# Pairs 0 and 1 share one seven-product T in the opening of an attention kernel on TensorE

## The chip, the cores and the metric

The kernel runs on one core of a Trainium2 chip. The metric is the device time of one execution in microseconds (us). TensorE multiplies, VectorE, ScalarE and GpSimd do the elementwise work, and SyncE issues the transfers.

## What is computed

```python
output = einsum('bni,io->bno', x, weight)              # x: (32, 256, 512) float32
q, k   = einsum('bni,io->bno', x, wq), einsum('bni,io->bno', x, wk)
alpha  = einsum('bno,bmo->bnm', q, k)
alpha  = softmax(maximum(alpha, 0) * (adj != 0), axis=1)
x      = layernorm(x + einsum('bnm,bmo->bno', alpha, output))
```

The kernel never forms q and k. It makes G = Wq Wk^T once, T = G x for each pair of batch elements, the scores x T, and V = x W.

## The kernel before

**Pairs, halves, splits.** The 32 batch elements are worked on as 16 pairs (a tile holds 2 x 256 rows). Each float32 operand is split into a rounded part `hi` and a rest `lo`, and a product is three matmuls: hi hi, hi lo, lo hi. The `hi` is a copy by ScalarE; the `lo` is a subtraction by VectorE (`rest`, line 1026) or GpSimd.

**Seven products.** A T or a V of 512 x 512 is made of 2 x 2 blocks by a seven-product scheme (`P1` to `P7`, each in two halves of six matmuls). It needs sums of x blocks (`xs`, S1 to S4, summed by GpSimd), their splits (`s_hi`, `s_lo`), sums of blocks of G (`T1` to `T3`, `D4`) or W, and sums over PSUM banks (`copy_t` on ScalarE, `sum_t` on VectorE).

**The loop.** From pair 2 on, a group works on two pairs. `fill_t` makes T for both at once: the x operand has 512 columns, 256 of each pair. Then come the output of the pair before, the scores of the first, its V, the scores of the second, the output of the first, and the second's V.

**The opening, which the change rewrites.** TensorE's list is: seven warm-up matmuls; `fill_first_v` (three of four rows of pair 0's V); `fill_g` (48 matmuls of 512 columns); `fill_first_t` (pair 0's T without the seven products: 48 matmuls of 512 columns); the fourth row of V; the scores of pair 0 (48 of 256 columns); `fill_second_t` (pair 1's T by seven products: 84 matmuls of 256 columns); the output of pair 0; the scores of pair 1; `fill_v(1)`; then the loop.

**The order on the other engines** is a list written out by hand for each engine. An engine runs its list strictly in order, and a semaphore wait at one operation holds back all behind it. The lists that matter here:
- ScalarE: splits of Wq and Wk, of V, of G, of x1 (pair 1's x) and its sums, of G's sums, of T; exponents of pair 0; copies of the second T among the roundings of p; T's splits; splits of pair 2's x and sums; exponents of pair 1; copies of V.
- VectorE: the rests of Wq and Wk, of V, of G, G's sums (`sum_gt`), their rests, T's, then masks and maxima, p's rests, the residuals of pair 0.
- GpSimd: waits for the last rest of Wk, then four x sums of pair 1, four rests of its x, four rests of its sums, four sums of W and their rests; four x sums of pair 2, its eight rests.
- SyncE: x0, W, Wq, Wk, the four blocks of x1 once x0 is split, adj; later x for the residual and pair 2.

Of the kernel before, what the change touches and what calls it, by code (L numbers as in the profile page):

```python
# [5 lines left out]
ALU = mybir.AluOpType  # L6
# [21 lines left out]
          (P5, 0): 9, (P5, 1): 10, (P3, 0): 11, (P3, 1): 12, (P4, 0): 13, (P4, 1): 14}  # L28
V_DONE = {(P1, 0): 1, (P1, 1): 2, (P7, 0): 3, (P6, 0): 4, (P6, 1): 5, (P7, 1): 6, (P5, 0): 7, (P5, 1): 8,
# [17 lines left out]
FIRST_A, FIRST_S = (A11, A21, A12, A22), (S3, S2, S1, S4)  # L47
# [6 lines left out]

B11, B12, B21, B22, T1, T2, T3, D4 = range(8)
W_ORDER = (T1, T3, T2, D4)
G_PLACE = {B11: 0, B21: 1, B22: 2, T1: 3, T2: 4, T3: 5, D4: 6}
# [3 lines left out]
def gnn_resnorm(nc: bass.Bass, x, x0_t, x_t, adj_t, w, wq_t, wk_t, out):  # L61
# [14 lines left out]
    with ExitStack() as ctx:  # L76
# [65 lines left out]
        wk_hi, wk_lo = a_hi[:, 1], a_lo[:, 1]  # L142
# [6 lines left out]
        b12 = parts[:, 0, 0]  # L149
# [16 lines left out]
        ring = [chain[:, 0], chain[:, 1], bank_y[:, 0], bank_y[:, 1]]  # L166
# [3 lines left out]
        g_bank = [o_bank[0], o_bank[1], o_bank[2], bank_z]  # L170
# [4 lines left out]
        xt_loaded, zeros_ready = sems("xt_loaded", 4), sem("zeros_ready")  # L175
# [13 lines left out]

        t_filled, t_copied, t_summed, c12_copied = sem("t_filled"), sem("t_copied"), sem("t_summed"), sem("c12_copied")  # L190
        v_filled, v_copied, v_summed = sem("v_filled"), sem("v_copied"), sem("v_summed")
        t0_filled, t_hi_ready, t_lo_ready = sem("t0_filled"), sem("t_hi_ready"), sem("t_lo_ready")
# [28 lines left out]
        def _(sp):  # L221
# [7 lines left out]
            def load_a(i, u):  # L229

                sp.wait_ge(x_summed[1], 4 * i - 4 + READ_BY[u])
                if u in B_LO_FIRST:
                    sp.wait_ge(b_lo_ready, 2 * i - 4 + B_LO_FIRST[u])
                else:
                    sp.wait_ge(a_lo_ready[1], 2 * i + A_LO[1][u])
                load_block(2 * i, u)

            def load_b(i, u):
                sp.wait_ge(x_summed[0], 4 * i - 4 + READ_BY[u])
                sp.wait_ge(a_lo_ready[0], 4 * i + A_LO[0][u])  # L240
                load_block(2 * i + 1, u)
# [76 lines left out]
        def _(pe):  # L318
# [16 lines left out]
            def t_half(i, c, pairs):  # L335
                to = {P2: bank_z[:, pairs], P7: bank_y[:, c, pairs], P4: bank_y[:, c, pairs]}.get(i, chain[:, c, pairs])
# [18 lines left out]
            def fill_t(i):  # L355
# [6 lines left out]
                def x_split(u):  # L362
                    pe.wait_ge(a_lo_ready[0], 4 * i + A_LO[0][u])
                    if u in B_LO_FIRST:
                        pe.wait_ge(b_lo_ready, 2 * i - 2 + B_LO_FIRST[u])
                    else:
                        pe.wait_ge(a_lo_ready[1], 2 * i + 2 + A_LO[1][u])

                def xs_split(s):
                    pe.wait_ge(s_lo_ready[0], 4 * i - 4 + S_LO[0][s])  # L370
                    pe.wait_ge(s_lo_ready[1], 4 * i + S_LO[1][s])
# [38 lines left out]
            def fill_second_t():  # L410

                def x_split(u):
                    pe.wait_ge(a_lo_ready[1], FIRST_A.index(u) + 1)

                def xs_split(s):
                    pe.wait_ge(s_lo_ready[1], FIRST_S.index(s) + 1)

                one = slice(1, 2)
                pe.wait_ge(gt_lo_ready, 4)
                xs_split(S3)  # L420
                t_half(P7, 0, one)
                x_split(A11)
                t_half(P1, 0, one)
                t_half(P1, 1, one)
                x_split(A12)
                t_half(P2, 0, one)
                t_half(P7, 1, one)
                pe.wait_ge(t_summed, 1)
                t_half(P2, 1, one)
                pe.wait_ge(t_copied, 1)  # L430
                xs_split(S2)
                t_half(P6, 0, one)
                pe.wait_ge(t_copied, 2)
# [12 lines left out]
                x_split(A22)
                t_half(P4, 0, one)
                pe.wait_ge(t_summed, 4)
                t_half(P4, 1, one)
# [57 lines left out]
            def fill_last_of_first_v():  # L507

                pe.wait_ge(gt_summed, 8)
# [5 lines left out]
            def g_chunk(j, k):  # L515
                half, cols = j // 2, slice(j % 2 * P, (j % 2 + 1) * P)
                return add_chunk(g_bank[j][:], (wq_hi[:, k, half, cols], wq_lo[:, k, half, cols]),
# [13 lines left out]

            def g_parts(k, j):
                kk, cols = k % 2, slice(j % 2 * P, (j % 2 + 1) * P)
                if k < 2 and j >= 2:
                    return p_hi[:, kk, cols], p_lo[:, kk, cols]
                b = G_PLACE[k // 2 * 2 + j // 2]
                return g_hi[:, b, kk, cols], g_lo[:, b, kk, cols]

            def fill_first_t():

                for k in range(K):
                    pe.wait_ge(g_lo_ready, (2, 4, 5, 6)[k])
                    h, kk = k // 2, k % 2
                    for j in range(K):
                        if k == 0 and j < R - 1:
                            pe.wait_ge(v_lo_ready, j + 1)
                        last = add_chunk(ring[j], g_parts(k, j), (a_hi[:, 0, h::2, kk], a_lo[:, 0, h::2, kk]),
                                         k == 0, k == K - 1)
                        if k == K - 1:
                            last.then_inc(t0_filled, 1)  # L550
# [20 lines left out]

            def fill_s_b(i):
# [4 lines left out]
                pe.wait_ge(a_lo_ready[1], 2 * i + 2 + A_LO[1][A21])  # L577
# [13 lines left out]
            def fill_o_b(i, first=False):  # L591

                p = 0 if first else 2 * i - 1
                for g in range(2):
                    pe.wait_ge(p_lo_ready, R * p + M * g + M)
                    if first:
                        pe.wait_ge(v_lo_ready, 4)
                    else:
                        pe.wait_ge(v_lo_ready, R * p + (V_AT[1][A11], 4)[g])
                        if g == 0:  # L600

                            pe.wait_ge(added, R * p)
                    for n in range(M):
                        if M * g + n == 3:
                            pe.wait_ge(added, R * p + 1)
                        fill_row(M * g + n, o_bank[(M * g + n) % 3][:])

# [65 lines left out]
        def _(act):  # L673
            def split_a(i, slot, u, first=False):

                act.wait_ge(xt_loaded[u], 32 * i + 16 * slot)
                if first:
                    act.wait_ge(s_filled, 2)
# [7 lines left out]
            def split_s(i, slot, s, first=False):  # L686
                act.wait_ge(x_summed[slot], 4 * i - 4 + 4 * slot + S_SUMMED[s])
# [15 lines left out]
            def copy_second_t(product):  # L703
                for c in range(2):
                    act.wait_ge(t_filled, T_DONE[product, c])
                    nc.scalar.copy(parts[:, PART[product], c, 1], chain[:, c, 1]).then_inc(t_copied, 1)
# [6 lines left out]
            def split_t_a(i, u):  # L713
                if u == A11:

                    act.wait_ge(s_filled, 4 * i)
# [8 lines left out]
            def copy_c12(i):  # L725

                act.wait_ge(squared, R * (2 * i - 1))
                nc.scalar.copy(c12_b[:], chain[:, :, 1]).then_inc(c12_copied, 1)

            def split_t_b(i, u):  # L730

                act.wait_ge(s_filled, 4 * i + 1 + u // 2)
                if u == A12:
                    act.wait_ge(c12_copied, i)
                whole = c12_b[:] if u == A12 else parts[:, BLOCK_AT[u], :, 1]
                nc.scalar.copy(t_hi[:, u], whole).then_inc(t_hi_ready, 1)

            def split_second_t(u):
                if u == A12:
                    act.wait_ge(t_filled, T_DONE[P3, 1])  # L740
                    whole = chain[:, :, 1]
                else:
                    act.wait_ge(t_summed, {A11: 2, A22: 4, A21: 6}[u])
                    whole = parts[:, BLOCK_AT[u], :, 1]
# [180 lines left out]
            def split_g(j):  # L925

                act.wait_ge(g_filled, j + 1)
                if j < 2:
                    nc.scalar.mul(g_hi[:, G_PLACE[B11], j], g_bank[j][:, 0], -1.0).then_inc(g_hi_ready, 1)
                    nc.scalar.mul(p_hi[:, j], g_bank[j][:, 1], -1.0).then_inc(g_hi_ready, 1)  # L930
                    if j == 0:
                        act.wait_ge(qk_lo_ready, 2 * K)
                    nc.scalar.mul(b12[:, j], g_bank[j][:, 1], -1.0).then_inc(b12_copied, 1)
                else:
                    b = G_PLACE[B21]
                    nc.scalar.mul(g_hi[:, b:b + 2, j - 2], g_bank[j][:], -1.0).then_inc(g_hi_ready, 1)
# [616 lines left out]
```

## Time and profile before

| | |
|---|---|
| time, median of 3 runs | 523.15 us (523.07 to 523.55) |
| the profiled execution's own time | 522.93 us |
| its span, first to last instruction | 521.1 us |
| TensorE busy | 511.5 us (98%), 3259 matmuls |
| VectorE, ScalarE, GpSimd busy | 370.8, 325.7, 257.4 us |
| mean granted TensorE clock | 0.996 of full |

The span is the time in which the profiler saw instructions; 1.8 us of the execution's time lie around it. Matmuls overlap, so the distance of their starts, not their duration, is what one costs.

### The profile page before, as it was taken

To read this page: it belongs to the slowest core of one execution; us is meant where nothing else is said; L and a number is where in the kernel's file an instruction comes from. 1 tells how busy PE (TensorE), PEld (TensorE's weight loads), DVE (VectorE), ACT (ScalarE), POOL (GpSimd) and SP (SyncE) were. 2 spreads that over 40 slices of the span, in tenths; PEclk is the share of its full clock that TensorE was granted. 3 is DMA by queue.
4 is the path that set the end of the run, shared out by engine and by line. 5 is a ranking of instruction groups with operands and counts; after the bars stand their busy time and mean duration, and the time that the engine had idled before them with its cause. 6 is when DMAs were issued, how large, how long until landed. Compare 5 with 4: busy or idle time off the path is not lost.

```text
span 521.1 us, 9934 instructions
## 1 busy us (share of the span) xinstructions
PE 511.5 (98%) x3259; PEld 466.4 (90%) x3259; DVE 370.8 (71%) x746; ACT 325.7 (62%) x747; POOL 257.4 (49%) x196
## 2 busy tenths in 40 slices
PE   8999999999999999999999999999999999999994
PEld 6889998899989998899988999889998999889994
DVE  5667845776948677586866778577684867757686
ACT  6566556386763857649474677638686385764583
POOL 0396974339535377145661486333952537810011
PEclk9999999999999999999999999999999999999998
DMA  8305231034330616024350343405251061502334
GB/s 304 140 1 192 79 136 61 21 141 143 129 134 20 221 61 241 20 65 177 122 199 20 121 141 128 154 20 182 100 200 61 20 221 60 201 1 67 135 135 187
DMA packets 30735, 62.05 MB, mean 119 GB/s; under 512 B 2048, under 2 KB 3072, under 8 KB 30720
## 3 DMA queue, kind: packets, MB, share of 16 engines
q1 hardware_dynamic: 30576, 61.61, 33.0%
q10 hardware_dynamic: 144, 0.26, 0.2%
q8 instruction: 7, 0.11, 0.1%
q14 instruction: 8, 0.07, 0.0%
HBM read 45.09 MB, written 16.78 MB: 119 GB/s over the span
## 4 chain that ended last, share of the span: by engine, by line
PE 95%; DVE 2%; ACT 1%; DMA 1%; issue 0%; POOLq 0%; POOL 0%; DVEq 0%; ACTq 0%
PE o_bank L320 12%; PE o_bank L321 12%; PE o_bank L322 12%; PE chain L320 11%; PE chain L322 11%; PE chain L321 11%; PE bank_y L320 6%; PE bank_y L321 6%; PE bank_y L322 6%; PE bank_z L320 3%; PE bank_z L322 3%; PE bank_z L321 3%; DMA xt<-in_x_t 1%; PE chain L502 0%; PE chain L503 0%; ACT v_hi L755 0%
## 5 line engine op out<-in xcount | busy, mean ns | idle before, releaser
L1442 POOL TENSOR_TENSOR s_lo<-xs,s_hi 128x512 fp32r<-128x512 f32 x60 | 82.0, 1384 | 35.4 <-ACT s_hi L692 35.4
L1437 POOL TENSOR_TENSOR a_lo<-xt,a_hi 128x512 fp32r<-128x512 f32 x42 | 58.3, 1396 | 61.5 <-ACT a_hi L684 61.5
L322 PE MATMUL o_bank<-t_hi,a_lo 128*128 128x256 f32 x256 | 72.4, 283 | 0.0
L321 PE MATMUL o_bank<-t_lo,a_hi 128*128 128x256 f32 x256 | 72.4, 283 | 0.0
L320 PE MATMUL o_bank<-t_hi,a_hi 128*128 128x256 f32 x256 | 72.4, 283 | 0.0
L1433 POOL TENSOR_TENSOR xs<-xt 128x512 f32<-128x512 f32 x30 | 39.1, 1318 | 45.6 <-DMA xt<-in_x_t 29.3
L1447 POOL TENSOR_TENSOR rstd<-var_eps,minus_half 128x4 f32<-128x4 f32 x14 | 14.2, 1015 | 92.6 <-DVE var_eps L1123 92.6
L711 ACT COPY parts<-chain 128x256 f32<-128x256 f32 x90 | 33.1, 369 | 39.6 <-PE chain L322 38.4
L320 PE MATMUL chain<-w_hi,s_hi 128*128 128x256 f32 x180 | 51.0, 284 | 0.5 <-ACT parts L711 0.5
L321 PE MATMUL chain<-w_lo,s_hi 128*128 128x256 f32 x180 | 50.9, 283 | 0.0
L322 PE MATMUL chain<-w_hi,s_lo 128*128 128x256 f32 x180 | 50.9, 283 | 0.0
L1026 DVE TENSOR_TENSOR v_lo<-parts,v_hi 128x512 fp32r<-128x512 f32 x45 | 48.8, 1097 | 0.9 <-ACT v_hi L755 0.9
L321 PEld LDWEIGHTS o_bank<-t_lo,a_hi 128*128 128x128 f32 x256 | 49.1, 192 | 0.3
L320 PEld LDWEIGHTS o_bank<-t_hi,a_hi 128*128 128x128 f32 x256 | 49.1, 192 | 0.3
L322 PEld LDWEIGHTS o_bank<-t_hi,a_lo 128*128 128x128 f32 x256 | 49.1, 192 | 0.0
L1038 DVE TENSOR_TENSOR parts<-parts,bank_y 128x512 f32<-128x512 f32 (+1 forms) x32 | 20.7, 653 | 39.2 <-ACT parts L701 26.1
L320 PE MATMUL o_bank<-v_hi,p_hi 128*128 128x512 f32 (+1 forms) x126 | 48.5, 385 | 0.0
L321 PE MATMUL o_bank<-v_lo,p_hi 128*128 128x512 f32 (+1 forms) x126 | 48.5, 385 | 0.0
L322 PE MATMUL o_bank<-v_hi,p_lo 128*128 128x512 f32 (+1 forms) x126 | 48.4, 384 | 0.0
L1109 DVE SCALAR_TENSOR_TENSOR xn<-o_bank,xn 128x512 f32<-128x512 f32 x60 | 41.0, 685 | 8.0 <-PE o_bank L322 8.0
L1129 DVE TENSOR_SCALAR xn<-xn,neg_mean,rstd 128x512 f32<-128x512 f32 x56 | 39.4, 725 | 10.1 <-POOL rstd L1447 10.1
L701 ACT COPY parts<-chain 128x512 f32<-128x512 f32 x42 | 24.6, 587 | 35.0 <-PE chain L322 34.4
(222 smaller groups left out, 1633.7 us busy)
## 6 DMA issues: line engine op xcount, KB each, us to landing
xt<-in_x_t SPq DMA_DIRECT2D x64, 256.0 KB, 3.1
xn<-in_x SPq DMA_DIRECT2D x16, 1024.0 KB, 5.2
out<-xn SPq DMA_DIRECT2D x14, 1024.0 KB, 6.0
adj<-in_adj_t SPq DMA_DIRECT2D x16, 512.0 KB, 5.5
xn<-in_wq_t SPq DMA_DIRECT2D x4, 256.0 KB, 5.2
parts<-in_wk_t SPq DMA_DIRECT2D x4, 256.0 KB, 5.2
out<-xn SPq DMA_DIRECT2D x2, 512.0 KB, 2.8
out<-xn SPq DMA_DIRECT2D x4, 256.0 KB, 2.3
```

What stands on the lines that cost most here:

```text
L320: nc.tensor.matmul(dst, a[0], b[0], start=first, stop=False, skip_group_check=shared)
L321: nc.tensor.matmul(dst, a[0], b[1], start=False, stop=False, skip_group_check=shared)
L322: return nc.tensor.matmul(dst, a[1], b[0], start=False, stop=last, skip_group_check=shared)
L701: nc.scalar.copy(parts[:, PART[product], c], chain[:, c]).then_inc(t_copied, 1)
L711: nc.scalar.copy(parts[:, PART[product], c, 0], chain_v[:, c]).then_inc(v_copied, 1)
L1026: return nc.vector.tensor_tensor(dst, whole, hi.bitcast(F32), ALU.subtract)
L1038: nc.vector.tensor_tensor(part, part, bank, ALU.add).then_inc(t_summed, 1)
L1109: nc.vector.scalar_tensor_tensor(out=xn[:, slot, r], in0=row.rearrange("q j n -> q (j n)"), scalar=1.0, in1=xn[:, slot, r], op0=ALU.mult, ...
L1129: nc.vector.tensor_scalar(xn[:, slot, r], xn[:, slot, r], neg_mean[:, r:r + 1], rstd[:, r:r + 1], ALU.add, ALU.mult).then_inc(normed, 1)
L1433: nc.gpsimd.tensor_tensor(xs[:, s], a, b, op).then_inc(x_summed[slot], 1)
L1437: nc.gpsimd.tensor_tensor(a_lo[:, slot, u], xt[:, u], a_hi[:, slot, u].bitcast(F32), ALU.subtract).then_inc(a_lo_ready[slot], 1)
L1442: nc.gpsimd.tensor_tensor(s_lo[:, slot, s], xs[:, s], s_hi[:, slot, s].bitcast(F32), ALU.subtract).then_inc(s_lo_ready[slot], 1)
```

## The change

Pair 0's dense T and pair 1's separate T go. Pairs 0 and 1 become the first group: one seven-product T of 84 matmuls of 512 columns, as in the loop. The rest of the opening follows the loop's order: scores of pair 0, the fourth row of V, scores of pair 1, output of pair 0, `fill_v(1)`. To feed it:
- pair 1's x lands in `soft` and a part of `parts`, behind Wk and with no wait; Wk's split is kept in pair 1's `s_hi`, `s_lo`; G's fourth row is in a half of `bank_y`, which leaves `bank_z` free;
- GpSimd makes x sums of both pairs from the sixth of the eight rests of Wq and Wk on; VectorE takes six of the rests that were GpSimd's (`split_first_b`, `split_first_s`);
- P2's second half goes to `o_bank0` in place of waiting for `bank_z`;
- the extra rounding of G's B12 (`p_hi`, `p_lo`) goes; G's last row is split as soon as it is filled, and G's sums and their splits are in the order T3, T2, T1, D4;
- pair 2's x is loaded, summed and its sums are rounded sooner: on ScalarE the four `split_s(1, 0, ...)` stand ahead of pair 1's `split_t_b`, and the roundings of its blocks stand between those of p.

```diff
+T_FIRST = {**T_DONE, (P1, 0): 1, (P1, 1): 2, (P2, 0): 3, (P2, 1): 4, (P7, 0): 5, (P7, 1): 6}
-FIRST_A, FIRST_S = (A11, A21, A12, A22), (S3, S2, S1, S4)
+FIRST_A, FIRST_S = (A11, A12, A22, A21), (S3, S1, S2, S4)
+FIRST_LO = {S3: 1, S2: 2}, {S1: 1, S4: 2}
+G_ORDER = (T3, T2, T1, D4)
...
+            def fill_first_t():
...
+                both = slice(0, 2)
+                pe.wait_ge(g_lo_ready, 2)
+                pe.wait_ge(b_lo_ready, B_LO_FIRST[A11])
+                pe.wait_ge(v_lo_ready, 2)
+                t_half(P1, 0, both)
+                t_half(P1, 1, both)
+                pe.wait_ge(g_lo_ready, 4)
+                pe.wait_ge(gt_summed, 1)
+                pe.wait_ge(b_lo_ready, B_LO_FIRST[A12])
+                t_half(P2, 0, both)
+                t_half(P2, 1, both, o_bank[0][:])
+                pe.wait_ge(gt_lo_ready, G_ORDER.index(T3) + 1)
+                xs_split(S3)
+                pe.wait_ge(v_lo_ready, 3)
+                t_half(P7, 0, both)
+                pe.wait_ge(gt_summed, 8)
+                t_half(P7, 1, both)
+                pe.wait_ge(t_copied, 1)
+                pe.wait_ge(gt_lo_ready, G_ORDER.index(T2) + 1)
+                xs_split(S2)
+                t_half(P6, 0, both)
...
+                pe.wait_ge(t_copied, 3)
+                pe.wait_ge(gt_lo_ready, G_ORDER.index(T1) + 1)
+                xs_split(S1)
+                t_half(P5, 0, both)
...
+                pe.wait_ge(t_copied, 5)
+                xs_split(S4)
+                t_half(P3, 0, both)
...
@@ TensorE's list @@
             fill_g()
             fill_first_t()
+            fill_first_s()
             fill_last_of_first_v()
-            pe.wait_ge(t_lo_ready, 4)
-            fill_scores(0, 0)
-            fill_scores(0, 1)
-            fill_second_t()
-            fill_o_b(0, first=True)
...
+            fill_s_b(0)
+            fill_first_o()
             fill_v(1, 1, first=True)
@@ ScalarE's list, the new one @@
+            split_first_a(A11)
+            split_first_s(0, S3)
+            split_first_a(A12)
+            split_g(0)
+            split_g(1)
+            split_first_s(0, S1)
+            split_first_s(0, S2)
+            split_first_a(A22)
+            split_first_a(A21)
+            split_g(2)
+            split_first_s(1, S3)
+            split_g(3)
+            split_gt(T3)
+            split_gt(T2)
+            split_first_s(1, S1)
+            copy_first_t(P1, 0)
+            copy_first_t(P1, 1)
+            split_first_s(0, S4)
+            split_first_s(1, S2)
+            split_gt(T1)
+            split_gt(D4)
+            split_first_s(1, S4)
+            copy_first_t(P6, 0)
+            copy_first_t(P6, 1)
+            split_t_a(0, A11, first=True)
+            copy_first_t(P5, 0)
+            copy_first_t(P5, 1)
+            split_t_a(0, A22)
+            split_t_a(0, A12)
+            copy_c12(0, first=True)
+            split_t_a(0, A21)
+            for b in W_ORDER[:-1]:
+                split_wt(b)
+            for s in (S2, S3, S1, S4):
+                split_s(1, 0, s, first=True)
+            split_t_b(0, A11)
+            split_t_b(0, A12)
+            exponent(0, 0)
+            exponent(0, 1)
+            split_t_b(0, A21)
+            exponent(0, 2)
+            exponent(0, 3)
+            split_t_b(0, A22)
+            split_first_v(R - 1)
+            for r, u in enumerate((A21, A11, A12, A22)):
+                split_a(1, 0, u, first=True)
+                split_p(0, r, first=True)
@@ VectorE's list, the new one @@
+            split_first_b(A11)
+            split_first_s(0, S3)
+            split_first_b(A12)
...
+            split_first_s(0, S2)
+            split_g(2)
+            sum_gt(T3, 0)
+            sum_gt(T2, 0)
+            split_g(3)
+            sum_gt(T3, 1)
+            split_first_s(1, S3)
+            split_gt(T3)
+            sum_gt(T2, 1)
+            sum_gt(D4, 0)
+            sum_gt(D4, 1)
+            split_gt(T2)
+            split_first_s(1, S2)
...
+            mask(0, 0, first=True)
+            relu_max(0, 0)
+            relu_max(0, 1)
+            split_t_b(0, A11)
+            mask(0, 1, first=True)
+            split_t_b(0, A12)
+            relu_max(0, 2)
+            relu_max(0, 3)
+            split_t_b(0, A22)
+            split_t_b(0, A21)
...
+            for r in range(R):
+                relu_max(1, r)
+            for r in range(R):
+                residual(0, 0, 0, r)
@@ GpSimd's list, the new one @@
+            pool.wait_ge(qk_lo_ready, 2 * K - 2)
+            sum_first_x(0, S3)
+            sum_first_x(0, S1)
+            sum_first_x(0, S2)
+            sum_first_x(1, S3)
+            split_first_s(0, S1)
+            sum_first_x(1, S1)
+            sum_first_x(0, S4)
+            sum_first_x(1, S2)
+            split_first_s(0, S4)
+            sum_first_x(1, S4)
+            split_first_s(1, S1)
+            split_first_s(1, S4)
+            split_first_a(A22)
+            split_first_a(A21)
...
             for s in (S3, S1, S2, S4):
                 sum_x(1, 0, s, first=True)
+            for b in W_ORDER[:-1]:
+                split_wt(b)
+            for s in (S2, S3, S1, S4):
+                split_s(1, 0, s)
             for u in (A21, A11, A12, A22):
                 split_a(1, 0, u)
+            split_wt(D4)
```

Between GpSimd's two parts stand the four sums of W, as before. `copy_first_t` of P5 waits for pair 1's A22 and A12 to be split, since they lie where P5's part goes.

## Rows read from the trace of the kernel before

**Rows 1.** The page: busy time of each engine, and TensorE by slices of the span.
```profile
PE 511.5 (98%) x3259; PEld 466.4 (90%) x3259; DVE 370.8 (71%) x746; ACT 325.7 (62%) x747; POOL 257.4 (49%) x196
...
PE   8999999999999999999999999999999999999994
...
PEclk9999999999999999999999999999999999999998
```

**Rows 2.** Waits of TensorE over the span: us in total, times, longest.
```profile
PE o_bank L650 <- DVE s_hi L1272: 1.5, 1, 1.5
PE chain L320 <- ACT parts L711: 0.5, 1, 0.5
```

**Rows 3.** Timeline of TensorE in the opening: start, duration, operation, shape.
```profile
24.63 0.39 PE L320 MATMUL chain<-a_hi,g_hi 128*128 128x512 f32 x1
...
35.51 0.39 PE L320 MATMUL o_bank<-w_hi,a_hi 128*128 128x512 f32 x1
...
38.23 0.28 PE L320 MATMUL o_bank<-t_hi,a_hi 128*128 128x256 f32 x1
...
43.98 0.28 PE L320 MATMUL bank_y<-s_hi,g_hi 128*128 128x256 f32 x1
...
54.53 0.40 PE L320 MATMUL o_bank<-v_hi,p_hi 128*128 128x512 f32 x1
...
65.75 0.28 PE L320 MATMUL chain<-w_hi,a_hi 128*128 128x256 f32 x1
...
68.61 0.38 PE L320 MATMUL chain<-w_hi,s_hi 128*128 128x256 f32 x1 [0.54 <-ACT parts L711]
```

**Rows 4.** Timeline of VectorE in the opening (xN: N in a row).
```profile
15.62 0.69 DVE L1026 TENSOR_TENSOR t_lo<-xn,t_hi 128x512 fp32r<-128x512 f32 x1
16.23 0.69 DVE L1026 TENSOR_TENSOR a_lo<-parts,a_hi 128x512 fp32r<-128x512 f32 x1
...
30.13 3.20 DVE L1026 TENSOR_TENSOR g_lo<-xn,g_hi 128x512 fp32r<-128x512 f32 x2 [1.99 <-ACT g_hi L940]
...
39.66 3.47 DVE L1026 TENSOR_TENSOR g_lo<-xn,g_hi 128x512 fp32r<-128x512 f32 x2
43.05 0.68 DVE L1082 SCALAR_TENSOR_TENSOR soft<-adj,o_bank 128x512 f32<-128x512 int32 x1
...
48.22 0.48 DVE L1099 SCALAR_TENSOR_TENSOR p_lo<-soft,inv_sum,p_hi 128x256 fp32r<-128x256 f32 x1 [0.66 <-ACT p_hi L771]
...
52.43 2.99 DVE L1026 TENSOR_TENSOR t_lo<-parts,t_hi 128x512 fp32r<-128x512 f32 x2
...
82.89 0.80 DVE L1099 SCALAR_TENSOR_TENSOR p_lo<-soft,inv_sum,p_hi 128x256 fp32r<-128x256 f32 x1
```

**Rows 5.** Timeline of GpSimd in the opening.
```profile
26.02 5.06 POOL L1482 TENSOR_TENSOR a_lo<-xt,a_hi 128x512 fp32r<-128x512 f32 x4 [3.62 <-ACT a_hi L971]
31.05 5.94 POOL L1442 TENSOR_TENSOR s_lo<-xs,s_hi 128x512 fp32r<-128x512 f32 x4
...
42.55 5.49 POOL L1498 TENSOR_TENSOR w_lo<-xn,w_hi 128x512 fp32r<-128x512 f32 x4
51.88 2.99 POOL L1433 TENSOR_TENSOR xs<-xt 128x512 f32<-128x512 f32 x2 [3.84 <-DMA xt<-in_x_t]
...
82.11 2.73 POOL L1442 TENSOR_TENSOR s_lo<-xs,s_hi 128x512 fp32r<-128x512 f32 x2 [1.63 <-ACT s_hi L692]
```

**Rows 6.** Timeline of ScalarE in the opening.
```profile
24.83 0.60 ACT L936 ACTIVATE g_hi<-bank_z 128x512 fp32r<-128x512 f32 x1 [2.12 <-PE bank_z L322]
25.32 2.17 ACT L971 CAST a_hi<-xt 128x512 fp32r<-128x512 f32 x4
...
44.23 0.51 ACT L763 ACTIVATE soft<-soft,neg_max 128x256 f32<-128x256 f32 x1 [0.99 <-DVE soft L1088]
```

**Rows 7.** Timeline of SyncE: x1's four loads.
```profile
9.95 1.76 SPq L226 DMA_DIRECT2D xt<-in_x_t  x4
```

**Rows 8.** The page's list of transfers: count, KB each, us to landing.
```profile
adj<-in_adj_t SPq DMA_DIRECT2D x16, 512.0 KB, 5.5
```

More of the change, by code:

```diff
@@ L141, in gnn_resnorm @@
         wq_hi, wq_lo = t_hi, t_lo
-        wk_hi, wk_lo = a_hi[:, 1], a_lo[:, 1]
+        wk_hi, wk_lo = s_hi[:, 1], s_lo[:, 1]
+        x1_raw = {A11: soft[:, 0:M], A21: soft[:, M:R], A12: parts[:, C22, 0], A22: parts[:, C22, 1]}
         def raw_block(raw, b):
@@ L530, in fill_g @@
                     last.then_inc(g_filled, 1)
[L532 to L550, printed above, removed]
             def fill_scores(slot, g):
@@ L701, in copy_t, with copy_first_t @@
                 nc.scalar.copy(parts[:, PART[product], c], chain[:, c]).then_inc(t_copied, 1)
[L703 to L706, printed above, removed]
+            def copy_first_t(product, c):
+                if product == P5:
+                    act.wait_ge(x_summed[1], 4)
+                    act.wait_ge(a_lo_ready[1], A_LO[1][A22])
+                    act.wait_ge(b_lo_ready, B_LO_FIRST[A12])
+                act.wait_ge(t_filled, T_FIRST[product, c])
+                nc.scalar.copy(parts[:, PART[product], c], chain[:, c]).then_inc(t_copied, 1)
             def copy_v(p, product, c):
@@ L733, in split_t_b @@
                 if u == A12:
-                    act.wait_ge(c12_copied, i)
+                    act.wait_ge(c12_copied, i + 1)
                 whole = c12_b[:] if u == A12 else parts[:, BLOCK_AT[u], :, 1]
[L736 to L744, printed above, removed]
                 nc.scalar.copy(t_hi[:, u], whole).then_inc(t_hi_ready, 1)
@@ L998, in _ @@
-            split_second_t(A12)
-            split_second_t(A21)
-            for u in (A21, A11, A12, A22):
-                split_a(1, 0, u, first=True)
+            split_first_s(1, S4)
[9 more added lines that the diff above has]
+            for b in W_ORDER[:-1]:
+                split_wt(b)
@@ L1030, in _, with sum_t @@
             COPIED = {P1: 0, P6: 2, P5: 4}
-            def sum_t(i, u, c, pairs=slice(0, 2)):
+            def sum_t(i, u, c, first=False):
                 product, copied = ADDED[u]
                 dve.wait_ge(t_copied, COPIES * i + COPIED[copied] + c + 1)
-                dve.wait_ge(t_filled, HALVES * i + T_DONE[product, c])
-                part = parts[:, BLOCK_AT[u], c, pairs]
-                bank = bank_z[:, pairs] if u == A11 else bank_y[:, c, pairs]
+                dve.wait_ge(t_filled, HALVES * i + (T_FIRST if first else T_DONE)[product, c])
+                part = parts[:, BLOCK_AT[u], c]
+                bank = bank_y[:, c] if u != A11 else o_bank[0][:] if first and c else bank_z[:]
                 nc.vector.tensor_tensor(part, part, bank, ALU.add).then_inc(t_summed, 1)
@@ L1313, in _ @@
+            split_first_v(R - 1)
             invert(0)
-            one = slice(1, 2)
-            sum_t(0, A11, 0, one)
             split_p(0, 0)
-            sum_t(0, A11, 1, one)
-            for r in range(1, R):
-                split_p(0, r)
-            sum_t(0, A22, 0, one)
-            sum_t(0, A22, 1, one)
-            split_second_t(A11)
-            split_second_t(A22)
-            sum_t(0, A21, 0, one)
-            sum_t(0, A21, 1, one)
-            split_second_t(A12)
-            residual(0, 0, 0, 0)
@@ L1328, in _ @@
-            residual(0, 0, 0, 1)
-            split_second_t(A21)
-            residual(0, 0, 0, 2)
-            residual(0, 0, 0, 3)
+            split_p(0, 1)
+            mask(1, 0)
+            split_p(0, 2)
+            split_p(0, 3)
+            mask(1, 1)
+            for r in range(R):
+                relu_max(1, r)
+            for r in range(R):
+                residual(0, 0, 0, r)
             means(0, first=True)
-            for g in range(2):
-                mask(1, g)
-                for r in range(g * M, (g + 1) * M):
-                    relu_max(1, r)
+            sum_v(1, A22)
```

300 lines of the change are left out of this document (145 added, 155 removed).

## Prediction

> **What bounds the kernel now.** I read the page first: TensorE is busy for 98% of the span, in every slice, at the full 2.4 GHz level of the granted clock [rows 1]. Then the waits: after the start TensorE waits for one thing only, a copy, 0.5 us [rows 2]. So the span is the sum of its matmuls, and a change of the opening acts in two ways: by matmul time taken off TensorE, and by holes that its suppliers leave in it. The timeline of TensorE gives the step from one start to the next: G ends and 48 wide matmuls run from 24.63 to 35.51, 0.2267 us each; 48 scores run from 38.23 to 43.98, 0.1198 us each [rows 3]. The old second T takes 10.55 us for 84 x 0.1198 = 10.06, and between 65.75 and 68.61 stand 18 matmuls of 256 columns, 2.16 us of work in 2.86, with 0.10 more lost right behind (0.22 to the next start where 0.12 is usual) [rows 3]: 0.80. The old opening thus holds some 1.3 us of holes.
>
> **What leaves TensorE.** Out: 48 x 0.2267 = 10.88 (pair 0's dense T) and 84 x 0.1198 = 10.06 (pair 1's T). In: 84 x 0.2267 = 19.04. That is -1.90 us. If no hole of the new opening opened, the old 1.29 would go too and `fill_v(1)` would start at 65.75 - 0.49 - 1.90 = 63.4.
>
> **What feeds it now.** The work of the suppliers has to fit a much tighter frame. Before, the second T had 20 us of other matmuls ahead of it. Now x sums and splits of *two* pairs must stand within the first T, the first scores follow T with nothing between, and each engine's list is strict. Prices: ScalarE 0.52 us per 512-wide split from SBUF (2.17 for 4), 0.60 to its result and 0.49 to the next from PSUM, 0.51 per exponent, its start 0.2 after the last matmul (24.83 for G's end at 24.63) [rows 3, 6]. GpSimd 1.25 to 1.27 per sum or split (5.06 for 4), [rows 5], and I add 0.1 where it waits for its own result. VectorE 0.61 per 512-wide split, 0.69 to its result [rows 4].
>
> That last price holds only while GpSimd rests. Two VectorE splits of G, both operands in SBUF, take 3.20 us instead of 1.3: the first, issued at 30.13, ends 0.55 after GpSimd's operation ends at 31.08; GpSimd's next then ends at 32.88 and the second split at 33.33. GpSimd's four take 5.94 instead of 5.06. The pair from 39.66 (3.47) and the pair from 52.43 (2.99) come out the same way, and p_lo at 82.89 takes 0.80 instead of 0.48. A mask, which reads PSUM, stays at 0.68 beside a busy GpSimd [rows 4, 5]. So the two take turns: a VectorE operation with two SBUF operands waits for GpSimd's current one (up to 1.25), then holds GpSimd up for 0.35 to 0.55. The Trainium skill ("SBUF — State Buffer", section "Who interferes with whom") says the same and speaks against this change: a VectorE instruction with two SBUF inputs contends with a GpSimd instruction that reads SBUF, under an exclusive lock. By the page's rule the sum is the one below; without it, that of the first rival. The trace agrees, 3.20 against 1.3.
>
> **The walk** (each start is an estimate: the previous one plus the prices above).
>
> G. GpSimd is released two splits earlier, near 15.75, while VectorE's splits of Wq and Wk stand back to back at 15.62 and 16.23 [rows 4]. It takes the second's turn: that one ends at 18.07 instead of 16.92, and G's last chunk, due at 17.83, waits **0.3**. G ends at 24.93.
>
> T, P6. GpSimd's sums and splits 1 to 8 last until 29.75. VectorE's slot-1 S3 split gets a turn at 27.95, T3's split only at 29.75, done at 30.3 (P7 is due at 30.37, hardly late). T2's sum is queued behind it (30.7), and on ScalarE behind that sum: T2's rounding, S1's, two copies of P1, S4's of slot 0, S2's of slot 1 = 3.2 us, to 33.9. VectorE's split of S2 then waits for GpSimd, which took S4 at 33.44: done 35.24. P6 is due at 33.1 and starts at 35.3: **2.2**. With every arbitration won it would be ready at 33.05.
>
> T, P5 and P3. P5 needs GpSimd's split of slot 1's S1 (38.29): **0.3**. The copy of P5 waits until GpSimd has split x1's A22 out of `parts` (five operations after 33.44, with three turns given away: 41.34), copy done 41.96; P3 is due at 41.07: **1.0**. T ends at 47.5.
>
> Scores of pair 0. First half not late (t_lo of A12 at 46.8). Second half waits for t_lo of A21, which gives GpSimd a turn: 50.63 for 50.37, **0.4**. V's last row covers until 56.3.
>
> Scores of pair 1. The edit that looks free is not: pair 2's four s roundings stand on ScalarE ahead of pair 1's t roundings, and the last waits for GpSimd's 22nd operation: 41.34 + 9 x 1.25 + own waits + 3 turns = 54.66. So ScalarE rounds t A11 at 55.4 to 56.0 and A12 by 56.5; VectorE, queued A11, mask, A12, waits two more turns: 59.5 for 56.3, **3.3**. The rest: the exponents wait for the maxima queued behind that split, t A22 is rounded at 61.5, VectorE's last two splits take two turns: 64.4 for 62.5, **1.9**.
>
> Output of pair 0. V's last split, inverse, p rounded from 65.1; the four p_lo each wait for one GpSimd split of pair 2's x (cadence 1.25 + 0.35 = 1.6): 67.2, 68.8, 70.4, 72.0. Row 0 is due at 67.3: **1.5**. Row 2 needs the fourth and mask(1,1), 72.65, for 71.6: **1.2**. Row 3 needs the residual, now behind four maxima, 74.8 for 74.1: **0.7**. `fill_v(1)` starts at 76.2; its last w_lo, GpSimd's 34th operation, is there at 73.3, and the exponents ahead of its first copy are over, so the old 0.80 is gone.
>
> Sum of holes 12.8. Against before: 76.2 - 65.75 - 0.80 = **+9.65 us**. What follows is as before: VectorE, ScalarE and GpSimd stand earlier against `fill_v(1)` than they did, so I cost it at nothing; if that cover were short it would show as a wait of the loop's first P7. The DMAs cost nothing either: x1 is four loads issued right behind Wk where the same four stood before [rows 7]; pair 2's loads follow by 28, pair 2's turn comes at 49; adj of pair 1 is issued near 58 with 5.5 us to land [rows 8] and is wanted at 69.
>
> **In numbers.** The profiled execution took 522.93 us with a span of 521.1; 522.93 + 9.65 = 532.6, and the median of the runs stands 0.22 above it: 532.8. What hides in the bold terms: each turn is worth 0 to 1.25 us, and about fourteen stand on the way to a hole, so the bounds are all of them nothing (the first rival) and all as walked.
>
> **Rivals.**
> 1. *The turns do not bite, and it is faster.* This is the one on the other side. With VectorE always at 0.69 the same walk gives T3's split at 28.35, P6's split at 32.45 for 32.8, P3 about 0.1 late, the 22nd operation at 49.5, scores(1) 0.35 and 0.5 late, row 3 0.4 late, `fill_v(1)` at 64.65: -1.1 - 0.8 = -1.9, 521.3. It decides where T3's split ends before 28.7. For it: most margins in that walk are 0.3 to 0.5 us, all positive. Against: [rows 4, 5] show the turns wherever both engines are busy.
> 2. *The turns bite in part.* If VectorE wins the turns in T, P6 to P3 lose 0.3 to 1 instead of 3.5, but GpSimd's total hardly shrinks: `fill_v(1)` at 74. If the p_lo fall into gaps as well, 3 us less again. 525.5 to 530.5; I take 528.5 as its middle. For it: x splits of pair 2 may be waiting for ScalarE when p is split.
> 3. *TensorE's clock falls.* No row shows it idle for over 1 us once it runs; a hole of 3.3 us is new. If it fell to the 1.2 GHz level for the 24 scores behind (2.9 us at full clock), up to 2.9 us more: 535.5. I take none.
> 4. *The wide T brings nothing that shows*: saving and holes cancel, 523. It would need the holes to come to 3.2 in all, between two walks that are 11 us apart.
>
> **Chances.** As walked, 531 to 534.5: 0.55. Rival 2: 0.24. Rival 1: 0.13. Rival 3: 0.05. Rival 4: 0.03. The likeliest is 532.8. The range that leaves out no more than 2 in 10 reaches through rival 2 to 525.5 and up to 534.8. A measurement of this kernel tells about 0.2% (1 us) from no change: faster 0.13, same 0.03, slower 0.84.
>
> **What would show it.** Right: TensorE waits at bank `chain` in T (P6), for s_lo or parts, 1 to 2.3 us; a wait of about 3 us ahead of the o_bank scores of pair 1; VectorE's splits between 20 and 72 at 1.1 to 1.8 us each where GpSimd is busy; 84 matmuls of 512 columns from 24.9. Wrong: `fill_v(1)` starts before 70, or VectorE's two-SBUF splits stay at 0.69 beside a busy GpSimd. The prediction falls if VectorE wins its turns, or if the ScalarE list runs ahead of GpSimd's sums of pair 2.

## The result, and the profile after

The changed kernel takes 531.42 us (median of 4 runs, 531.0 to 531.76) against 523.35 (4 runs, 523.07 to 523.66) for the kernel before: ratio 1.0154, 95% interval 1.0142 to 1.0165, slower by 8.1 us. The forecast was 532.8 us, or 9.65 more than before.

The page of the changed kernel: 48 matmuls fewer (3211 for 3259), and TensorE's row has lost three nines near the start, and the fifth slice has a lower granted clock, where [rows 1] has nines up to the last slice (an 8 in both).

```profile
PE 513.3 (97%) x3211; PEld 463.9 (88%) x3211; DVE 379.6 (72%) x750; ACT 328.8 (62%) x750; POOL 263.8 (50%) x198
...
PE   8989789999999999999999999999999999999994
...
PEclk9999899999999999999999999999999999999998
```

The waits of TensorE (us in total, times, longest). From 12 us on the kernel before has one wait, of 0.5 us [rows 2]. Now there are eight (the one of 1.5 us for s_hi belongs to the start), and the engine named is VectorE in six:

```profile
PE o_bank L329 <- DVE t_lo L1050: 2.9, 1, 2.9
PE chain L329 <- DVE s_lo L1050: 1.6, 1, 1.6
PE o_bank L667 <- DVE s_hi L1294: 1.5, 1, 1.5
PE o_bank L329 <- DVE p_lo L1118: 1.0, 1, 1.0
PE o_bank L329 <- DVE soft L1101: 0.6, 1, 0.6
PE chain L329 <- ACT parts L719: 0.6, 1, 0.6
PE o_bank L329 <- issue: 0.3, 1, 0.3
PE o_bank L329 <- DVE xn L1128: 0.2, 1, 0.2
PE o_bank L329 <- DVE s_lo L1050: 0.2, 1, 0.2
```

The timeline of TensorE gives their places: G's last chunk, P6, P3, the scores of pair 1 (their first start, two starts at the lower clock, and the second half), rows 0, 2 and 3 of the output, and the start of `fill_v(1)`, which was at 65.75 in [rows 3]:

```profile
18.35 0.50 PE L329 MATMUL o_bank<-s_hi,t_hi 128*128 128x512 f32 x1 [0.23 <-DVE s_lo L1050]
...
35.22 0.47 PE L329 MATMUL chain<-s_hi,g_hi 128*128 128x512 f32 x1 [1.61 <-DVE s_lo L1050]
...
41.70 0.50 PE L329 MATMUL chain<-s_hi,g_hi 128*128 128x512 f32 x1 [0.55 <-ACT parts L719]
...
58.87 0.39 PE L329 MATMUL o_bank<-t_hi,a_hi 128*128 128x256 f32 x1 [2.88 <-DVE t_lo L1050]
...
60.48 0.42 PE L329 MATMUL o_bank<-t_hi,a_hi 128*128 128x256 f32 x1
60.70 0.41 PE L330 MATMUL o_bank<-t_lo,a_hi 128*128 128x256 f32 x1
...
63.55 0.43 PE L329 MATMUL o_bank<-t_hi,a_hi 128*128 128x256 f32 x1 [0.31 <-issue]
...
67.71 0.47 PE L329 MATMUL o_bank<-v_hi,p_hi 128*128 128x512 f32 x1 [0.99 <-DVE p_lo L1118]
...
71.30 0.47 PE L329 MATMUL o_bank<-v_hi,p_hi 128*128 128x512 f32 x1 [0.60 <-DVE soft L1101]
...
73.17 0.50 PE L329 MATMUL o_bank<-v_hi,p_hi 128*128 128x512 f32 x1 [0.24 <-DVE xn L1128]
...
74.65 0.28 PE L329 MATMUL chain<-w_hi,a_hi 128*128 128x256 f32 x1
```

74.65 - 65.75 is 8.90; less the 0.80 that the kernel before lost just behind that point, 8.10, and the spans stand at 529.2 and 521.1. So all of the change lies ahead of `fill_v(1)`.

VectorE's timeline shows the turns. An operation with two SBUF operands takes 0.69 in [rows 4] where GpSimd rests; here single ones take 1.78 (the last rest of Wk, which G's last chunk waits for), 1.77 (T3's rest of G), 1.34 (pair 1's S2), 1.73 and 1.15 (pair 1's t_lo), and the p_lo, 0.48 each there, take 2.76 and 2.16 for two:

```profile
16.52 1.78 DVE L1050 TENSOR_TENSOR s_lo<-parts,s_hi 128x512 fp32r<-128x512 f32 x1
...
28.41 1.77 DVE L1050 TENSOR_TENSOR g_lo<-xn,g_hi 128x512 fp32r<-128x512 f32 x1
30.11 0.41 DVE L1279 SCALAR_TENSOR_TENSOR xn<-bank_y,xn 128x256 f32<-128x256 f32 x1
...
33.73 1.34 DVE L1050 TENSOR_TENSOR s_lo<-xs,s_hi 128x512 fp32r<-128x512 f32 x1 [1.83 <-ACT s_hi L959]
...
55.41 1.73 DVE L1050 TENSOR_TENSOR t_lo<-parts,t_hi 128x512 fp32r<-128x512 f32 x1 [3.48 <-ACT t_hi L752]
...
57.66 1.15 DVE L1050 TENSOR_TENSOR t_lo<-c_b,t_hi 128x512 fp32r<-128x512 f32 x1
...
64.80 2.76 DVE L1118 SCALAR_TENSOR_TENSOR p_lo<-soft,inv_sum,p_hi 128x256 fp32r<-128x256 f32 x2 [0.66 <-ACT p_hi L778]
...
68.27 2.16 DVE L1118 SCALAR_TENSOR_TENSOR p_lo<-soft,inv_sum,p_hi 128x256 fp32r<-128x256 f32 x2
```

GpSimd's timeline gives the other side. The first two sums take 3.38, where two took 2.5: the first started while VectorE was in a rest, and the last rest of Wk then waited for it. S4 of slot 0 (pair 0; slot 1 is pair 1) starts at 33.26 after 3.62 us without work, ahead of VectorE's S2 at 33.73, which ends 0.54 after it.

```profile
16.07 3.38 POOL L1479 TENSOR_TENSOR xs<-xt 128x512 f32<-128x512 f32 x2 [15.23 <-DVE s_lo L1050]
...
28.07 1.56 POOL L1479 TENSOR_TENSOR xs<-xs,soft 128x512 f32<-128x512 f32 x1
33.26 1.27 POOL L1483 TENSOR_TENSOR s_lo<-xs,s_hi 128x512 fp32r<-128x512 f32 x1 [3.62 <-ACT s_hi L959]
...
52.81 1.29 POOL L1503 TENSOR_TENSOR xs<-xt,xs 128x512 f32<-128x512 f32 x1 [0.17 <-POOL xs L1503]
54.07 4.20 POOL L1574 TENSOR_TENSOR w_lo<-xn,w_hi 128x512 fp32r<-128x512 f32 x3
58.23 6.37 POOL L1512 TENSOR_TENSOR s_lo<-xs,s_hi 128x512 fp32r<-128x512 f32 x4
```

ScalarE's timeline: T2's rounding at 30.55 after an idle of 2.17 that ends with T2's sum, and pair 2's s roundings up to 54.85, the last behind GpSimd's sum of 52.81, ahead of pair 1's t roundings:

```profile
30.55 0.62 ACT L944 CAST g_hi<-xn 128x512 fp32r<-128x512 f32 x1 [2.17 <-DVE xn L1279]
...
52.67 2.18 ACT L701 CAST s_hi<-xs 128x512 fp32r<-128x512 f32 x4 [2.23 <-POOL xs L1503]
54.76 0.62 ACT L752 CAST t_hi<-parts 128x512 fp32r<-128x512 f32 x1
```

### The profile page after: what moved, and what is told of

It is laid out like the page before. It is cut to its first block, busy times and chain, and to the rows that moved or that the text cites. A ratio compares the mean times of both kernels' runs of the same rounds, so it can differ in the third digit from the quotient of the medians.

```text
span 529.2 us, 9835 instructions
## 1 busy us (share of the span) xinstructions
PE 513.3 (97%) x3211; PEld 463.9 (88%) x3211; DVE 379.6 (72%) x750; ACT 328.8 (62%) x750; POOL 263.8 (50%) x198
## 4 chain that ended last, share of the span: by engine, by line
PE 83%; DVE 2%; ACT 1%; issue 0%; POOLq 0%; POOL 0%; DVEq 0%; ACTq 0%
PE chain L330 10%; PE chain L331 10%; PE chain L329 10%; PE o_bank L329 10%; PE o_bank L330 10%; PE o_bank L331 10%; PE bank_y L329 5%; PE bank_y L330 5%; PE bank_y L331 5%; PE bank_z L330 2%; PE bank_z L331 2%; PE bank_z L329 2%; DVE p_lo L1118 0%; ACT v_hi L762 0%; DVE xn L1392 0%
## 5 line engine op out<-in xcount | busy, mean ns | idle before, releaser
L1512 POOL TENSOR_TENSOR s_lo<-xs,s_hi 128x512 fp32r<-128x512 f32 x56 | 77.9, 1408 | 40.2 <-ACT s_hi L701 40.2
L1062 DVE TENSOR_TENSOR parts<-parts,bank_y 128x512 f32<-128x512 f32 x32 | 21.9, 686 | 42.6 <-ACT parts L710 25.8
L1503 POOL TENSOR_TENSOR xs<-xt 128x512 f32<-128x512 f32 x28 | 36.4, 1310 | 26.1 <-DMA xt<-in_x_t 26.1
L1050 DVE TENSOR_TENSOR v_lo<-parts,v_hi 128x512 fp32r<-128x512 f32 x45 | 47.6, 1069 | 0.9 <-ACT v_hi L762 0.9
```

What stands on the lines that cost most here:

```text
L1050: return nc.vector.tensor_tensor(dst, whole, hi.bitcast(F32), ALU.subtract)
L1062: nc.vector.tensor_tensor(part, part, bank, ALU.add).then_inc(t_summed, 1)
L1503: nc.gpsimd.tensor_tensor(xs[:, s], a, b, op).then_inc(x_summed[slot], 1)
L1512: nc.gpsimd.tensor_tensor(s_lo[:, slot, s], xs[:, s], s_hi[:, slot, s].bitcast(F32), ALU.subtract).then_inc(s_lo_ready[slot], 1)
```

## The experiments

The theory: VectorE's operations with two SBUF operands and GpSimd's take turns; in the new opening both engines are busy, the turns make rests late, and the strict lists of ScalarE and VectorE carry each delay on to TensorE. The rivals: the order of the lists alone would do it; or GpSimd's total is the bound, so that no order helps; or an operation with one operand makes the kernel faster for another reason than the turns. A hole is what a start of TensorE is later than the step of 0.2267 or 0.1198 us allows; the sums below count them from 12 to 90 us: 11.2 us in the changed kernel (the 1.1 us of its matmuls at the lower clock among them), 1.3 in the kernel before. What is lost ahead of 12 us isn't in them. It differs from one profiled execution to the next: beyond what the holes explain, T's first matmul starts 0.1 to 1.2 us later than in the profile of the kernel before.

**one_operand**: the changed kernel without the turns. VectorE's operation leaves out the subtraction of `hi`, so its second operand; waits, order and matmuls stay.

```diff
+            def rest_1(dst, whole, hi=None):
+                k = next(at)
+                return nc.vector.tensor_scalar(dst, whole, 0.0, None, ALU.min, ALU.min, accum_out=spare[:, k:k + 1])
...
-                rest(g_lo[:, G_PLACE[b]], g_sum(b), g_hi[:, G_PLACE[b]]).then_inc(gt_lo_ready, 1)
+                rest_1(g_lo[:, G_PLACE[b]], g_sum(b), g_hi[:, G_PLACE[b]]).then_inc(gt_lo_ready, 1)
```

and so for the rests of x1, of both pairs' sums, of t (all but pair 0's A12, which it reads from PSUM), of p, and the last of Wq and Wk: 23 operations (the expectation counts 24).

> The changed kernel; in the opening VectorE's 24 rests with two SBUF operands are replaced by an operation of the same shape with one SBUF operand (lo = min(whole, 0), so lo parts of pairs 0 and 1 and of G's sums are wrong); every wait, order and matmul stays. If the turns between VectorE and GpSimd are the cause (my theory): the holes go, all but some tenths at P3, scores of pair 1 and row 3; 521.3 to 522.5 us, and VectorE's replaced operations stay at 0.7 beside a busy GpSimd. If the order of the lists alone is the cause (rival): the holes stay, 529 to 531.5.

Measured: 522.38 us, ratio to before 0.9976 (0.9966 to 0.9986). The holes come to 1.8 us. All that TensorE waits for after 12 us:

```profile
PE o_bank L330 <- issue: 0.2, 1, 0.2
PE o_bank L330 <- DVE t_lo L1055: 0.2, 1, 0.2
```

T3's rest of G and pair 1's t A12 on VectorE, and GpSimd's rests of W and of pair 2's sums at the same time:

```profile
28.57 0.69 DVE L1055 TENSOR_SCALAR_CACHE_REDUCE g_lo<-xn 128x512 fp32r<-128x512 f32 x1
...
53.26 0.68 DVE L1055 TENSOR_SCALAR_CACHE_REDUCE t_lo<-c_b 128x512 fp32r<-128x512 f32 x1
```

```profile
50.70 3.80 POOL L1581 TENSOR_TENSOR w_lo<-xn,w_hi 128x512 fp32r<-128x512 f32 x3
54.46 5.04 POOL L1519 TENSOR_TENSOR s_lo<-xs,s_hi 128x512 fp32r<-128x512 f32 x4
```

1.15 has become 0.68, and GpSimd's three and four rests take 3.80 and 5.04 where they took 4.20 and 6.37. Nothing else was touched, and 9.0 us went. That an accumulating `tensor_scalar` does not contend is also what the Trainium skill says ("SBUF — State Buffer", section "Who interferes with whom"); the 0.68 beside a busy GpSimd agrees. The rival "order alone" falls.

**before_one_operand**: the control, the same replacement in the kernel before, where TensorE had cover.

```diff
-                rest(g_lo[:, G_PLACE[b]], g_sum(b), g_hi[:, G_PLACE[b]]).then_inc(gt_lo_ready, 1)
+                rest_1(g_lo[:, G_PLACE[b]], g_sum(b), g_hi[:, G_PLACE[b]]).then_inc(gt_lo_ready, 1)
```

and so for three blocks of the second T and for pair 0's p, 11 operations.

> A control: the kernel before, with the same replacement in its opening (the rests of G's sums, of three blocks of the second T and of pair 0's p read one SBUF operand, so those lo parts are wrong). My theory: TensorE hardly waited for these there, so the replacement itself is worth nothing: 523.2 to 523.6 us, at most the 0.5 us of holes in the second T less. If a one-operand operation made the kernel faster by itself (rival to the reading of the other run): 521 or less.

Measured: 523.63 us, ratio 1.0005 (0.9995 to 1.0015), holes 1.36 for 1.34. Here the operation by itself gives nothing; it gives 9 us only where the turns reach TensorE.

**act_mid**: ScalarE's wait for T2's sum is filled.

```diff
             split_gt(T3)
-            split_gt(T2)
             split_first_s(1, S1)
             copy_first_t(P1, 0)
             copy_first_t(P1, 1)
             split_first_s(0, S4)
             split_first_s(1, S2)
+            split_gt(T2)
```

> The changed kernel; on ScalarE the rounding of G's T2 moves behind the two copies of P1 and three roundings of x sums, which don't need it. Theory: ScalarE's 2.2 us of waiting for T2's sum is used; GpSimd's split of slot 0's S4 starts near 30.6 instead of 33.3, the hole at P6 falls from 1.8 to 0.8, those at P5 and P3 go; later holes stay, since GpSimd and TensorE move together: 529.4 us (2.0 less than the change). Rival, that the copy and rounding order is without effect because GpSimd's total sets the time: 531.4.

Measured: 529.53 us, ratio 1.0112 (1.0095 to 1.0129), 1.9 less than the change. The hole at P6 is 0.72 with 0.07 behind it, those at P5 and P3 are gone, and the later ones stand as they were (3.04 ahead of pair 1's scores). As expected (529.4); the rival of the total falls for this place.

**act_late**: pair 2's s roundings behind what pair 1's scores wait for.

```diff
-            for s in (S2, S3, S1, S4):
-                split_s(1, 0, s, first=True)
             split_t_b(0, A11)
             split_t_b(0, A12)
             exponent(0, 0)
             exponent(0, 1)
             split_t_b(0, A21)
+            split_t_b(0, A22)
             exponent(0, 2)
             exponent(0, 3)
-            split_t_b(0, A22)
+            for s in (S2, S3, S1, S4):
+                split_s(1, 0, s, first=True)
             split_first_v(R - 1)
```

> The changed kernel; on ScalarE pair 2's four s roundings move behind pair 1's t roundings and pair 0's exponents, and t A22 is rounded ahead of the last two exponents. Theory: the 3.1 us hole ahead of pair 1's scores shrinks to 0.3, some 1 us of it comes back ahead of their second half (VectorE's last two rests still take turns), TensorE's clock doesn't fall there: 528 us (3.4 less), between 527.5 and 529. Rival, GpSimd's total sets the time: 531.4.

Measured: 528.57 us, ratio 1.0093 (1.0076 to 1.0109), 2.9 less than the change where 3.4 were expected. Both holes at pair 1's scores are gone, 5.0 us of them with the lower clock. A new one is there, which stood in neither theory at this size: `fill_v(1)` waits for GpSimd's last rest of W.

```profile
PE chain L329 <- POOL w_lo L1574: 1.8, 1, 1.8
```

In the profiled execution the clock falls behind it: from 73.85 on 15 matmuls of 256 columns are 0.213 us apart and cost 1.4 us that no later wait takes back. That execution is the longest of the four, 530.09 at a mean granted clock of 0.993; the other three, at 0.996, took 528.19 to 528.94. So the rival about GpSimd's total is true here: once TensorE runs ahead, GpSimd's 34th operation is late.

**pool_2k**: GpSimd released after the eighth rest again.

```diff
-            pool.wait_ge(qk_lo_ready, 2 * K - 2)
+            pool.wait_ge(qk_lo_ready, 2 * K)
```

> The changed kernel; GpSimd is released after the eighth rest of Wq and Wk again, not after the sixth. Theory: the hole of 0.49 in G goes, GpSimd's first operation starts at 17.4 instead of 16.6 (after its turn), and later holes take the 0.5 back: 531.0 to 531.8, no difference that can be told. Rival, that the early release costs what it shows in G: 530.9; that it gains what it moves GpSimd ahead: 532.3.

Measured: 531.46 us, ratio 1.0152 (1.0135 to 1.0169), the change's own 531.42. G has no hole, P2 has one of 0.24 and P6 one of 2.17 for 1.84. The early release neither costs nor gives: it moves 0.5 us.

**both**: `act_mid` and `act_late` together.

> The changed kernel with both reorderings of ScalarE's list. Theory: the two gains act at different places and GpSimd, 2 us ahead by the first, no longer holds fill_v(1) up: 2.0 + 2.9 less than the change, 526.3 us (525.8 to 527). Rival, GpSimd's total sets the time: not under 528.5.

Measured: 526.57 us, ratio 1.0069 (1.0053 to 1.0086). The gains add (1.9 and 2.9), but not for the reason given: `fill_v(1)` still waits 1.7 us for w_lo, since TensorE is ahead by as much as GpSimd. Behind that wait the clock doesn't fall in the profiled execution (526.11); the longest of the four runs, 527.74, has the lower mean clock, 0.992 for 0.996.

**both_quiet**: `both`, and GpSimd without work while p is split. ScalarE's list, against that of `both`:

```diff
-            for s in (S2, S3, S1, S4):
-                split_s(1, 0, s, first=True)
             split_first_v(R - 1)
-            for r, u in enumerate((A21, A11, A12, A22)):
-                split_a(1, 0, u, first=True)
-                split_p(0, r, first=True)
             split_wt(D4)
+            for r in range(R):
+                split_p(0, r, first=True)
+            for s in (S2, S3, S1, S4):
+                split_s(1, 0, s, first=True)
+            for u in (A21, A11, A12, A22):
+                split_a(1, 0, u, first=True)
```

On GpSimd D4's rest of W stands behind the other three.

> Both reorderings, and ScalarE rounds pair 2's s and x blocks behind pair 0's p, so that GpSimd has nothing to do while VectorE makes p_lo; GpSimd makes D4's rest of W ahead of pair 2's rests. Theory: the holes of 1.2 and 0.8 at rows 0 and 2 of the output go: 524.3 us (523.8 to 525). Rival: GpSimd's eight rests, 3 us later, hold up the loop's first T instead: 526 and a wait at the loop's first P7 or P1.

Measured: 524.04 us, ratio 1.0017 (1.0004 to 1.003), 2.5 less than `both`. The waits for p_lo, for the mask and for w_lo are gone. The profiled execution, the longest of the ten at 527.69, shows the rival's wait at the loop's first P7. GpSimd has waited for pair 3's loads twice just before:

```profile
PE bank_y L329 <- POOL s_lo L1512: 2.0, 1, 2.0
```

```profile
73.62 1.29 POOL L1503 TENSOR_TENSOR xs<-xt 128x512 f32<-128x512 f32 x1 [1.74 <-DMA xt<-in_x_t]
...
76.39 1.57 POOL L1503 TENSOR_TENSOR xs<-xt 128x512 f32<-128x512 f32 x1 [1.48 <-DMA xt<-in_x_t]
```

Behind the wait seven wide matmuls are 0.43 us apart. The hole of 2.2 and these 1.4 come to 3.6 us; this execution is 3.65 above the median.

**both_quiet_res**: the same, `pool_2k`, and pair 0's first residual ahead of pair 1's maxima.

```diff
+            residual(0, 0, 0, 0)
             for r in range(R):
                 relu_max(1, r)
-            for r in range(R):
+            for r in range(1, R):
                 residual(0, 0, 0, r)
```

> The same, with pair 0's first residual ahead of pair 1's maxima on VectorE, and GpSimd released after the eighth rest of Wq and Wk. Theory: the hole of 0.5 at row 3 goes and that of 0.5 in G moves or goes: 523.4 us (523 to 524.3). Rival: row 3 was covered by the others and nothing changes: 524.3.

Measured: a median of 523.93 us, ratio 1.0041 (1.0011 to 1.0072): inconclusive for so small an edit, since its ten runs lie between 523.11 and 529.61 where the kernel before has 522.91 to 523.88, and the few long ones pull the ratio above what the median says. In its profiled execution (523.23) row 3 has no hole; P6 has 1.04, row 2 0.84, P7 0.50.

**ahead**: that one, with pair 2's x blocks ahead of its sums on ScalarE and GpSimd, and all p_lo ahead of pair 1's masks on VectorE.

> The last version, with two more moves: ScalarE and GpSimd take pair 2's x blocks ahead of its sums, so that pair 3's loads start 5 us sooner, and VectorE makes all four p_lo ahead of pair 1's masks, while GpSimd still waits. Theory: the hole of 0.84 at row 2 goes, that of 0.6 at the loop's first P7 (GpSimd waits for pair 3's loads) goes; what stays is 1.0 at P6: 521.8 us (521.3 to 522.4), under both kernels, and with less spread. Rival: GpSimd has no slack left and a new wait takes their place: 523.3 or more.

Measured: 523.13 us (522.16 to 525.68, 12 runs), ratio 1.0005 (0.9991 to 1.0019). In the profiled execution (522.54) both holes are gone, but 0.64 came up at the second half of pair 0's scores. The expectation, 521.8 and under both kernels, is missed by 1.3: the fastest runs are under the kernel before, the ratio isn't.

**ahead_6**: the same with `2 * K - 2`.

> The same, but GpSimd released after the sixth rest of Wq and Wk, as in the change. Theory: the early release trades 0.5 in G for the same at P6, no difference over 0.3 us: 521.6 to 522.2. Rival, that it costs what it shows in G: 522.3.

Measured: 524.01 us (522.12 to 526.04, 12 runs), ratio 1.0012 (0.9997 to 1.0028), above both figures expected. It differs from `ahead` by 0.9 in the median, the intervals overlap, the fastest are 0.04 apart. The profiles agree with "no difference" (holes 2.15 and 2.41); the medians can't decide.

**ahead_t**: `ahead`, rearranged within T.

```diff
-            split_first_s(0, S4)
             split_first_s(1, S2)
+            split_first_s(0, S4)
             split_gt(T2)
@@ VectorE @@
             sum_gt(T2, 1)
+            split_first_s(1, S2)
             sum_gt(D4, 0)
             sum_gt(D4, 1)
             split_gt(T2)
-            split_first_s(1, S2)
```

D4's rest of G moves behind the sums of A22 on VectorE, and x1's A22 ahead of the last sum's rest on GpSimd.

> The version ahead, and within T: slot 1's S2 is rounded and split before GpSimd can start on slot 0's S4, D4's rest of G stands later on VectorE, and GpSimd splits x1's A22 ahead of the last sum. Theory: the 1.0 at P6 goes, 0.3 to 0.5 comes back at P5 or P3: 0.6 less than ahead, 521.2 to 522.5 us, clear of the kernel before by 0.2%. Rival: P3 takes all of it back: 522.2 to 523.2. If the runs of this version spread over 3 us as those of the last two did, it's not the holes in T that spread.

Measured: 522.73 us (522.24 to 523.72, 11 runs), ratio 0.9988 (0.9979 to 0.9997). No hole is left at P6, P5 and P3; 1.13 and 0.61 stand at the scores of pair 0. It is faster than the kernel before by 0.1%, with the interval just clear of 1. That it gains on `ahead` isn't shown: the holes are 2.65 for 2.41 in the profiled executions, and what P6 gave back came up at the scores, not at P5 or P3 as expected. Its runs spread over 1.5 us instead of 3.5, but they were taken on another chip than those of `ahead`, so the order of T is not shown to be what narrowed them.

## Why the prediction was right

The prediction's reading of the page holds: TensorE is the bound, and the change is what it adds up to there. The saving of 1.90 us is not seen by itself, but the span of `one_operand`, 520.5 with 1.8 us of holes, is what it leaves: 521.1 - 1.34 - 1.90 + 1.82 = 519.7, and in that execution T's first matmul started 0.83 us later (25.46, with no hole ahead of it from 12 us on) than in [rows 3] (24.63), which makes 520.5.

The walk, hole by hole, in us:

| place | predicted | measured |
|---|---|---|
| G's last chunk | 0.3 | 0.49 |
| P6 | 2.2 | 1.84 |
| P5 | 0.3 | 0.20 |
| P3 | 1.0 | 0.81 |
| scores of pair 0, second half | 0.4 | 0.07 |
| scores of pair 1, first half | 3.3 | 3.14 |
| scores of pair 1, second half | 1.9 | 1.9 (1.12 at the lower clock, 0.75 wait) |
| output row 0 | 1.5 | 1.23 |
| output row 2 | 1.2 | 0.84 |
| output row 3 | 0.7 | 0.52 |
| sum | 12.8 | 11.0 |

- **The turns.** Shown by `one_operand` against its control. T3's rest of G ended at 30.18 (predicted 30.3), S2's at 35.07 (35.24), pair 1's t A12 at 58.81 (59.5).
- **The lists.** Both that the prediction named were moved, and their holes went with them. Neither cause does it alone: without the turns the same lists cost under 2 us of holes; with the turns, another order (`ahead_t`) takes 8.5 of the 11.2 away.
- **What was too large.** The holes came to 11.0 us and not 12.8, and 0.25 us more lie outside the table's places, so that the whole is 1.55 over (9.65 against 8.1). The largest part is at the output (2.6 instead of 3.4), and there the price of a turn was too high. The walk lets each p_lo hold GpSimd up by 0.35; GpSimd's five rests from 64.56 to 71.56 took 7.00 where the same five took 6.31 in `one_operand`, 0.17 per p_lo. With p rounded from 64.17 on (walked: 65.1), the fourth p_lo ended at 70.43 instead of 72.0. What made the smaller excesses at P6, P3 and the scores wasn't taken apart.
- **Rival 3, the clock.** It did fall: 12 scores of pair 1 from 60.48 on are 0.213 us apart instead of 0.1198. It was priced at up to 2.9 us more and cost nothing that shows: the second half had to wait for t_lo until 63.45 in any case, and the fall took 1.12 us of that wait. The run whose mean granted clock was 0.996 took 531.45 us, those at 0.992 took 531.0 and 531.39. The prediction gave it a time of its own and forgot that the next stop was already late.
- **Cover that was costed at nothing.** Behind `fill_v(1)` the changed kernel loses nothing, as predicted. The cover was thin though: in `act_late` and `both` GpSimd's last rest of W is 1.7 to 1.8 us late, in `both_quiet` pair 3's S3.

What stays open: why the runs of `both_quiet`, `both_quiet_res`, `ahead` and `ahead_6` spread over 3.5 to 6.5 us where both kernels spread over 1. Two parts are seen. In the one long execution that was profiled, the wait at P7 and the stretch at the lower clock behind it are as large as the excess. And the longest runs of `both_quiet` and `both_quiet_res` (526.88 to 529.61) have a mean granted clock of 0.989 to 0.995, the others 0.995 to 0.998. In `ahead` and `ahead_6` the clock doesn't tell them apart: runs at 0.995 took from 522.2 to 525.8. Which wait those lost their time to wasn't seen.

## What to carry to other kernels

Before work is shifted to VectorE or GpSimd to feed a faster matmul order, count the operations with two SBUF operands that will meet a busy GpSimd, and price each at the other's remaining time on top of its own; utilisation rows (72% and 50% here) don't show it. Where an engine's list is strict, put what the bound engine wants next ahead of what merely is ready sooner, and look at which engine's wait the early item brings along. When a stall is removed, look for the next one right away: here `act_late`, `both` and `both_quiet` each met a supplier that had been hidden by the stall itself.

## What the runs showed of the hardware

- The turns alternate. At 16.07 GpSimd came while VectorE was in one rest (15.91 to 16.60) with another queued; that rest kept its 0.69, and GpSimd's first sum went between the two (3.38 for two sums, 1.78 for the queued rest). A rest of 512 elements holds GpSimd up by 0.3 to 0.5 us in these timelines, a p_lo of 256 elements by some 0.17 (an estimate, from the five rests above).
- In the profiled executions a stretch at the lower of TensorE's two clock levels (granted clock 0.50 between 60.4 and 62.8) came after waits of 2.9 us (12 matmuls; also in `act_mid` and `pool_2k`), 1.8 us (`act_late`) and 2.0 us (`both_quiet`), but not after 1.6 at P6, nor after 1.9 there in `pool_2k`, nor after 1.7 in `both`. So these waits don't sort by length alone. Where the next operand was late anyway it was free; in `act_late` it cost 1.4 us.
- An accumulating `tensor_scalar` on 512 elements takes the time of a plain rest (0.68 for 0.69) and is not held up by GpSimd (`one_operand`).
